# Four more experts computed in the transposed form, and a steadier issue of the first state tile's preparation

## The reference

```python
x = x + 0.5 * ffn(layernorm(x), ...)       # kind 0
x = x + mamba(layernorm(x), ...)           # a state-space layer
x = x + 0.5 * ffn(layernorm(x), ...)       # kind 1, the same weights
```

```python
cw  = normalised product of two softmaxes over the experts   # [token, e]
h   = silu(x @ w_gate[e]) * (x @ w_up[e])                    # 128 -> 512
out = sum over e of cw[:, e] * (h @ w_down[e])               # 512 -> 128
```

## Time and profile before

| | us |
|---|---|
| median of 3 runs | 1242.97 |
| lowest, highest | 1241.31, 1243.07 |
| the profiled execution | 1242.44 |
| its span | 1240.6 |

### The profile page before, as it was taken

One profiled execution on the slowest core, in us unless ns is written; L12 is line 12 of the kernel. 1 busy time (PEld: TensorE's weight loads), 2 busy tenths in 40 slices (PEclk: granted clock), 3 DMA queues, 4 the chain that ended last, 5 costly groups with the idle time before them and its releaser, 6 DMA issues.

```text
span 1240.6 us, 20186 instructions
## 1 busy us (share of the span) xinstructions
PE 1233.1 (99%) x7072; PEld 1058.2 (85%) x7072; DVE 1143.4 (92%) x1368; ACT 1003.6 (81%) x2122; POOL 446.4 (36%) x571
## 2 busy tenths in 40 slices
PE   9999999999999999999999999999999999999999
PEld 7787788888888888888888888888888888887887
DVE  6958899999999999999999999997999999978877
ACT  7678789798898898988879898797988978846654
POOL 1021134445453463453434434452444344402000
PEclk9999999999999999999999999999999999999999
DMA  8412458888788997987889887986688979932322
GB/s 227 111 27 45 105 116 174 165 171 167 162 176 178 183 187 157 198 170 165 181 180 187 166 196 160 191 181 138 131 166 169 196 169 194 182 63 43 74 48 60
DMA packets 121015, 184.84 MB, mean 149 GB/s; under 512 B 11344, under 2 KB 38096, under 8 KB 120912
## 3 DMA queue, kind: packets, MB, share of 16 engines
q0 software_dynamic: 53568, 97.54, 45.0%
q1 hardware_dynamic: 67344, 86.00, 26.6%
HBM read 83.30 MB, written 2.69 MB: 69 GB/s over the span
## 4 chain that ended last, share of the span: by engine, by line
PE 93%; DVE 3%; ACT 2%; issue 1%; DMA 1%; SPq 0%; DVEq 0%; ACTq 0%
PE PS L1105 28%; PE PS L996 19%; PE PS L999 18%; PE PS L997 18%; PE PS L1101 2%; PE PS L1097 2%; PE PS L1099 2%; PE PS L1163 1%; PE PS L1148 1%; DVE HB L1345 1%; PE PS L1032 1%; DVE HL L1301 1%; PE PS L1040 1%; DMA YE<-CWD 1%; PE PS L1003 0%
## 5 line engine op out<-in xcount | busy, mean ns | idle before, releaser
L1105 PEld LDWEIGHTS PS<-WD,HB 128*128 128x128 f32 x3200 | 393.9, 191 | 22.1 <-issue 2.0
L1105 PE MATMUL PS<-WD,HB 128*128 128x128 f32 x3200 | 395.9, 275 | 0.0
L1345 DVE TENSOR_TENSOR HB<-PS,HB 128x1024 f32<-128x1024 f32 (+1 forms) x336 | 322.9, 962 | 72.5 <-PE PS L999 56.7
L1555 ACT ACTIVATE HB<-PS 128x512 f32<-128x512 f32 x512 | 294.9, 596 | 95.5 <-PE PS L999 93.5
L1733 POOL DMA_DIRECT2D Y<-HS x252 | 221.8, 954 | 317.6 <-DMA Y<-HS 151.7
L996 PE MATMUL PS<-XH,WG 128*128 128x512 f32 x509 | 219.7, 432 | 0.3 <-ACT HB L1555 0.2
L996 PE MATMUL PS<-XH,WU 128*128 128x512 f32 x512 | 204.4, 399 | 0.4 <-DVE HB L1345 0.4
L999 PE MATMUL PS<-XH,WU 128*128 128x512 f32 x512 | 201.2, 393 | 0.0
L999 PE MATMUL PS<-XH,WG 128*128 128x512 f32 x509 | 200.7, 394 | 0.1
L997 PE MATMUL PS<-XH,WU 128*128 128x512 f32 x512 | 200.4, 391 | 0.0
L997 PE MATMUL PS<-XH,WG 128*128 128x512 f32 x509 | 199.3, 392 | 0.0
(11 more groups left out here) (164 smaller groups left out, 1572.9 us busy)
## 6 DMA issues: line engine op xcount, KB each, us to landing
BCB<-BCD SPq DMA_DIRECT2D x128, 512.0 KB, 5.2
Y<-HS POOLq DMA_DIRECT2D x252, 256.0 KB, 6.0
XT<-YE POOLq DMA_DIRECT2D x99, 256.0 KB, 5.1
YE<-CWD SPq DMA_DIRECT2D x27, 256.0 KB, 4.5
AT<-YE POOLq DMA_DIRECT2D x21, 256.0 KB, 3.3
WD<-in_L_ffn_w_down_dram SPq DMA_DIRECT2D x8, 256.0 KB, 6.0
XT<-in_L_attn_x_dram SPq DMA_DIRECT2D x7, 256.0 KB, 5.8
out_dram<-XT SPq DMA_DIRECT2D x7, 256.0 KB, 5.4
```

Of the source, the lines that this page charges most:

```text
L1105: z = pe.matmul(part(g, j), HB[:, i % NH, j * P:(j + 1) * P], WD[:, e, c, :], start=c == 0 and j == 0, stop=c == FC - 1 and j == SUB - 1)
L1345: v.tensor_tensor(H, PS[:, NG + i % 2:NG + i % 2 + n, :], H, ALU.mult).then_inc(S["v_h"], 1)
L1555: a.activation(HB[:, i % NH, :], gate(i), ACT.Silu).then_inc(S["a_sil"], 1)
```

## The change

`TURNS` gets expert 0 of position 1, so that all eight of it are turned, and experts 5 to 7 of position 13; 31 turned experts in place of 27. `SPLITS`, `TURN_BEGINS`, `TURN_ENDS` and the lists worked out from `TURNS` follow. `HURRY` is 1, so that `side()` advances `before` once at each call until the first scan stream has begun, whatever the planned DVE clock is; `fill()` may advance it again after that.

```diff
-HURRY = 0
+HURRY = 1
...
-TURNS = {0: range(1, 6), 1: range(1, 8), 14: range(0, 8), 15: range(0, 7)}
+TURNS = {0: range(1, 6), 1: range(0, 8), 13: range(5, 8), 14: range(0, 8), 15: range(0, 7)}
```

## The result

The changed kernel takes 1260.22 us (median of 4 runs, 1258.65 to 1261.41), the kernel before 1242.55 beside it: a ratio of 1.0143 [1.0125, 1.0161], 17.7 us slower. I had forecast 1240.0, with slower at 0.22. The profiled execution took 1261.41, its span is 1259.6 against 1240.6, so the traces have 19.0 us to explain.

A forecast was written before the change was run, and what follows sets the result against it. PE was taken as the bound, a row of matmuls with hardly a gap. The terms −3.2 + 0.6 + 0.2 + 0.2 − 1.2 + 0.4 gave −3.0 us, to 1240.0 us, with a range of 1237.8 to 1246.8.

The forecast's parts named there:

- Down products: In the 16 slots of the four newly turned experts: 0.20 us less per slot, −3.2 us in all.
- transposes: Position 13 newly needs four transposes of AT and one of cw on PE: +0.6 us.
- Rows of weights: Position 1, expert 0's first weight row: DVE waits 0 to 1 us for it; +0.2 us, bounds 0 and +1.0.
- Handing AT from position 13 to 14: Position 14's first product into AT must follow position 13's transposes, so DVE can wait; +0.2 us, bounds 0 and +1.0.
- The stall at slot 63: End of position 1: PE's wait for HL behind a scan operand goes; −1.2 us, bounds −1.4 and 0.
- The steadier issue: The flag brings state tile 0's preparation and scans forward from position 1 on, costing nothing by itself.
- head start: State tile 0's scans start up to 10 us earlier, bounds 0 and 14.3.
- Rival D: The flag does nothing, scans start at 154 as before and position 13 pays; 0.24 together with another rival.
- Scans among turned slots: Some 15 scan instructions among turned slots of positions 1 and 13, mostly hidden; +0.4 us, bounds 0 and +5.
- 22 us of slack: Position 13's last scans can move behind, with 22 us before position 15's normalisation, twice what is pushed.
- Rival B: DVE sets the pace of position 13's last 12 slots: +3.4 to +6.4 us, 1246.4 to 1249.4; milder 1243 to 1246; chance 0.22.

The follow-up runs named there:

- hurry: Kernel before with HURRY = 1 alone, 27 turned experts as before: 1257.87 us, ratio 1.0124.
- p13: Kernel before with only experts 5 to 7 of position 13 turned, HURRY = 0: 1256.81 us, ratio 1.0108.
- turns: Kernel before with all 31 turned experts of the change but HURRY = 0: 1254.08 us, ratio 1.0101.
- p13h: Kernel before with HURRY = 1 and experts 5 to 7 of position 13 turned, not expert 0 of position 1: 1270.94 us, ratio 1.0229.
- block8: Kernel before with eight unused 128 × 512 additions on DVE ahead of the product of expert 6 of position 1: 1250.85 us, ratio 1.0065.
- block4: Kernel before with four unused 128 × 512 additions on DVE ahead of the product of expert 6 of position 1: 1247.62 us, ratio 1.0036.
- after_both: Changed kernel, expert 6's row load ahead of the broadcasts, position 1's weights transpose, store and first row load right behind slot 34's down product: 1250.03 us.
- operand_later: Kernel before with state tile 0's second scan operand moved behind HL of slot 63 on DVE: 1241.96 us, ratio 0.9989.
- p1_both: Kernel before with expert 0 of position 1 turned, HURRY = 0, its first weights early and a row load ahead of the broadcasts: 1250.17 us, ratio 1.0050.

## Why the prediction was wrong

- **Down products, −3.2, transposes, +0.6.** Right in count. In time position 13 agrees: it got 2.3 to 3.6 us shorter, 1.8 of the 3.6 being a projection that moved on, which leaves the 1.8 forecast for three experts. With 2.6 us of work saved, what the new order costs is 17.7 + 2.6 = 20.3, eight times as much.
- **Rows of weights, "DVE waits 0 to 1 us there", +0.2.** Mis-sized, and its premise false. I left the store and the load at the times of the kernel before; the planner moved them 3.4 and 5.5 us later, and the store itself landed after 3.6 us, not 1.4. DVE waited 4.2 us, and the move forward gave 3.4 back. The bound should have included a new place for the load.
- **Handing AT from position 13 to 14, +0.2.** Nothing of it came: the transposes stand at 1126.63 and DVE's first product into AT at 1134.86, without a wait.
- **The stall at slot 63, −1.2.** The size agrees with what was measured alone (−1.34, with an interval from −0.4 to −2.5), but in the changed kernel the place got worse, 5.9 in place of 1.2. I took the load behind it to land in the 4.4 us of the earlier trace rows, though that was a median, and the row of the kernel before behind the same three broadcasts took 9.6. This is the largest single failure, 6.8 us; no step of the sum had it.
- **The steadier issue, "It costs nothing by itself".** The step that failed most plainly: the flag alone costs 14.9 us. The instructions are the same, but their places are not, and 6.4 us of it is that another row fell behind the broadcasts. The head start of up to 10 us was 1.6 us in hurry, and in the changed kernel the scans came 18 us later. Rival D had it that the scans do not come earlier, but gave the flag no cost.
- **Scans among turned slots, +0.4, bounds 0 and +5; "22 us of slack, twice what is pushed".** The slack was counted against one later user. But the tile's closing fell among the turned slots of position 14: its gate, at 1097.40 before, stands at 1156.18 in the changed kernel, 59 us later, and PE waits 2.3 us behind it; in p13 it came as a burst, and PE waits 6.55. Rival B named the engine and the sign, put the place at the end of position 13 and a price of 3.4 to 6.4 on it; measured alone it is 13.5 us, at the next position. In the changed kernel a part of that is spared (+5.4 in position 14). That is the work of expert 0 of position 1 and not of the flag: turns spares it too, p13h, which has the flag without that expert, does not.
- **Common to all:** I priced a wait at its length. Behind three waits of the changed kernel, 2.2, 5.9 and 2.3 us long, PE ran at a lower clock, and in block8 and block4 a us of DVE's lateness cost 1.3 to 1.5.

What stays open: after_both is still 6.9 us slower than the kernel before. Its trace has as waits 2.3 us for HL in position 14, with a granted clock of 0.67 over the 5 us from 1147, 1.7 for h behind the end of position 1, and 1.8 for XN in later positions; no run here divides the rest among them.

## What to carry to other kernels

Where a planner writes the order, a change in its input is a new order for all engines: cost it only after listing which steps change places, and for each queue what now stands ahead of a small transfer or an instruction that others wait behind. Take a transfer's landing time from the transfer that stood in the same company in the trace, not from the median. In a kernel whose PE has no gap, a saving of tenths a slot is smaller than one wait of 4 us, so move single steps first (operand_later) and let the large changes come after.

## What the runs showed of the hardware

- A 256 KB broadcast load issued 1.4 us after three of 512 KB on SP's queue landed after 12.9 us (changed kernel), 11.2 (hurry) and 9.6 (before); issued ahead of them after 4.5. A DMA of another queue near them is slow too: a sum into AT, issued by POOL within 3 us of them, took 11.5 us in the changed kernel, 10.7 in p1_both and 9.0 in after_both, where 3.3 is the median. The Trainium skill ("DMA: Bandwidth & Descriptors", Queues, rings and completion order) has descriptors of one ring taken up in order, and each DMA engine going round between the rings it has work for, a packet at a time; both agree with these rows, where the load behind the three on SP's queue lands last and the transfer on POOL's is slowed beside them; no run here shows the rings themselves.
- The granted clock fell while PE still waited: in block8 it was 0.90 over 159 to 166, with the wait of 7.0 us ending at 166.47, then 0.61 over the next 7 us and 1.00 after. It was 0.68 over 7 us behind a wait of 5.9 (changed kernel) and 0.57 over 4 us around one of 4.1 (block4). Matmuls over 512 columns start 0.42 us apart in the low stretch in place of 0.23; the two levels are 1.2 and 2.4 GHz.
- The length of the wait alone does not tell: behind a wait of 2.3 us at nearly the same place of position 14 the clock was 0.57 over 4 us in the changed kernel and 1.00 in turns.
